# Softplus evictions gathered at the end of step 8, two products put later, one more tile on VectorE, and fewer rows of xh

## The reference, cut to what matters

```
xh, z = split(x @ W_in)                 # 512 channels each
xc = depthwise_conv_3x3(xh)             # 'SAME' padding
dt_r, Bp, Cp = split(xc @ W_xproj)      # 8, 16, 16
dt = softplus(dt_r @ W_dt + b_dt)       # 512 channels
dtN = dt @ W_dtN + b_dtN                # 16 states
for each pixel t, each channel, each of 16 states n:
    h[n] = exp(dt * A[n]) * h[n] + dtN[n] * Bp[n] * xc
    y    = sum over n of h[n] * Cp[n]  + Dskip * xc
y = layernorm(y) * silu(z) @ W_out + b_out
```

## Time and profile before

| what | value |
|---|---|
| time, median of 3 runs | 4421.09 us (4414.24 to 4431.68) |
| the profiled execution: its time, its span | 4415.12 us, 4413.4 us |
| VectorE busy | 4047.4 us, 92% of the span |
| GpSimd busy | 3843.1 us, 87% |
| TensorE busy | 3540.8 us, 80% |
| ScalarE busy | 3411.3 us, 77% |
| mean granted clock of TensorE | 0.922 |
| scan, L1041, 1536 of them | 2731.6 us |
| activation table loads, 385 of them | 1283 ns each |

### The profile page before, as it was taken

The page is one execution under the profiler, slowest core; times in us unless marked ns, Lnnn a source line. Parts: engine busy times, 40 slices in busy tenths (PEclk is TensorE's granted clock), DMA queues, the critical chain, the costliest instruction groups (busy, mean ns, idle before and its releaser), DMA issues.

```text
span 4413.4 us, 64194 instructions
## 1 busy us (share of the span) xinstructions
PE 3540.8 (80%) x20244; PEld 2225.9 (50%) x20244; DVE 4047.4 (92%) x4017; ACT 3411.3 (77%) x5782; POOL 3843.1 (87%) x2518
## 2 busy tenths in 40 slices
PE   6787888888887788877888778887887788878876
PEld 3454555555555555545554555454554555445544
DVE  3999999999999999999999999999999999999996
ACT  4778787777877787777787777887787777878774
POOL 4999999889998899888999889988899888998894
PEclk8899999998999999999899999999999899999987
DMA  5233223322233223322232223222232223222310
GB/s 132 65 97 100 65 69 100 91 87 62 85 92 92 79 61 103 91 79 75 83 102 73 79 72 101 86 75 76 89 105 65 75 82 105 83 61 80 100 54 22
DMA packets 189295, 363.22 MB, mean 82 GB/s; under 512 B 27416, under 2 KB 164120, under 8 KB 188960
## 3 DMA queue, kind: packets, MB, share of 16 engines
q1 hardware_dynamic: 188960, 359.12, 27.7%
HBM read 289.84 MB, written 69.21 MB: 81 GB/s over the span
## 4 chain that ended last, share of the span: by engine, by line
DVE 26%; ACT 23%; PE 20%; issue 18%; POOL 12%; DVEq 0%; DMA 0%; POOLq 0%; ACTq 0%; SPq 0%
DVE st L1041 18%; POOL st L599 10%; PE ht L1190 8%; ACT decay L727 6%; DVE y L1017 3%; ACT L918 3%; ACT weighed L756 3%; PE work L1227 2%; ACT dt L799 2%; ACT L799 2%; PE work L1262 2%; PE work L1232 1%; PE work L1163 1%; ACT xb L878 1%; PE work L1222 1%
## 5 line engine op out<-in xcount | busy, mean ns | idle before, releaser
L1041 DVE TENSOR_TENSOR_SCAN st<-decay,st 128x1024 f32<-128x1024 f32 (+1 forms) x1536 | 2731.6, 1778 | 138.6 <-ACT decay L727 101.0
L599 POOL TENSOR_TENSOR st<-xc,bbc 128x1536 f32<-128x1536 f32 x768 | 2652.0, 3453 | 56.1 <-DMA bbc<-brow 46.9
L727 ACT ACTIVATE decay<-dt,neg_a 128x1024 f32<-128x1024 f32 (+1 forms) x1536 | 1356.8, 900 | 413.4 <-DVE st L1041 410.7
L1190 PE MATMUL ht<-ident,st 128*128 128x128 f32 x9216 | 1348.5, 297 | 337.1 <-DVE st L1041 299.9
L1190 PEld LDWEIGHTS ht<-ident,st 128*128 128x128 f32 x9216 | 1134.6, 153 | 648.8 <-DVE st L1041 465.1
L1017 DVE SCALAR_TENSOR_TENSOR y<-ht,ct,y 128x512 f32<-128x512 f32 x1536 | 1119.9, 729 | 89.8 <-PE ht L1190 89.4
L632 POOL TENSOR_TENSOR y<-y,weighed 128x512 f32<-128x512 f32 x672 | 854.4, 1271 | 340.3 <-ACT weighed L756 336.1
L756 ACT ACTIVATE weighed<-ht,ct 128x512 f32<-128x512 f32 x672 | 459.4, 684 | 274.1 <-PE ht L1190 271.7
L1227 PE MATMUL work<-xn,win 128*128 128x384 f32 x768 | 344.6, 594 | 136.7 <-DVE volt L997 103.2
L1163 PE MATMUL work<-tri,conv_w 96*32 96x384 f32 x4608 | 415.6, 493 | 5.2 <-issue 2.0
L1222 PE MATMUL work<-xn,win 128*128 128x480 f32 x768 | 359.9, 593 | 4.6 <-ACT xn L850 3.2
(11 more groups left out here) (109 smaller groups left out, 3173.2 us busy)
## 6 DMA issues: line engine op xcount, KB each, us to landing
bbc<-brow SPq DMA_DIRECT2D x192, 768.0 KB, 6.1
tri<-rows_of_xh SPq DMA_DIRECT2D x576, 200.0 KB, 3.9
rows_of_xh<-xhp SPq DMA_DIRECT2D x192, 250.0 KB, 2.4
out_dram<-ot SPq DMA_DIRECT2D x43, 384.0 KB, 4.2
xin<-in_x_dram SPq DMA_DIRECT2D x42, 384.0 KB, 3.4
st<-in_x_dram SPq DMA_DIRECT2D x6, 384.0 KB, 5.5
out_dram<-y SPq DMA_DIRECT2D x4, 384.0 KB, 2.6
brow<-xp SPq DMA_DIRECT2D x48, 24.0 KB, 1.5
```

The lines of the kernel that those rows point to most:

```text
L599: u = g.tensor_tensor(slot, xc[:, kq % 2, :, :], bbc[:, piece_slot(kq, p), n % PIECE, :].unsqueeze(1).to_broadcast([P, DC, T]), ALU.mult)
L727: a.activation(flat(decay[:, :, :])[:, lo:hi], flat(dt[:, (k + ahead) % 2, :, :])[:, lo:hi], ACT.Exp, scale=neg_a[:, n:n + 1]).then_inc(s_ ...
L1041: v.tensor_tensor_scan(state[:, lo:hi], flat(decay[:, :, :])[:, lo:hi], state[:, lo:hi], 0.0 if h == 0 else state[:, lo - 1:lo], ALU.mult, ...
L1190: last = t.transpose(ht[:, m, c * P:(c + 1) * P], st[:, j, c, m * P:(m + 1) * P], ident[:, :])
```

## The change

- The four softplus evictions stand together at the end of step 8 with one pair of table loads. The products dt0 and dt1 stay at the end of step 7; dt2 and dt3 go to step 9, behind its transposes and ahead of l0 and l1.
- State 8 joins the table `OWN`: its tile 2 goes to VectorE.
- The first of the two membrane copies in step 9 stands ahead of `next_decay`.
- `TIN_STEPS` is (0, 6) in place of (6, 8).
- A chunk's xh is made only for the 8 rows that the chunk before did not have (384 columns), except for an image's first chunk, with 10. Rows in DRAM are kept for a whole image, and the normalised input xn loses a row that nothing reads.

```diff
-TIN_STEPS = (6, 8)
+TIN_STEPS = (0, 6)
...
-OWN = (10, 11,)
+OWN = (8, 10, 11,)
...
     7: ([(PRE, "ct")], [(PRE, "dt0"), (PRE, "dt1")], []),
-    8: ([], [(PRE, "dt2"), (PRE, "dt3")], []),
+    9: ([], [], [(PRE, "dt2"), (PRE, "dt3")]),
...
-                sp.dma_start(rows_v[c], xhp[:, c % 3, :, :].rearrange("p r w -> p (r w)")).then_inc(s_put[c], 16)
+                kq = (k + 1) % K
+                r0 = 0 if kq == 0 else TAPS - 1
+                sp.dma_start(rows_v[c][:, (kq * ROWS + r0) * WP:((kq + 1) * ROWS + 2) * WP],
+                             xhp[:, c % 3, r0:, :].rearrange("p r w -> p (r w)")).then_inc(s_put[c], 16)
...
-                    r0, r1 = (W if kx == 0 else 0), (HALO - W if kx == K - 1 else HALO)
+                    r0, r1 = W, (HALO - W if kx == K - 1 else HALO)
...
+                    taken = [(kc, h) for kc, a0_step in (L1_SLOTS.get(k, ()) if L1 in do else ())
+                             for h in range(CH) if s == l1_step(a0_step, h)]
+                    if s == BOTH_AT:
+                        for kc, h in taken[:1]:
+                            copy_membrane(kc, h)
                     next_decay(s)
...
+                    for kc, h in taken[1:] if s == BOTH_AT else taken:
+                        copy_membrane(kc, h)
                     for kind, name in late:
-                        if kind in do:
+                        if kind in do and name[:2] != "dt":
                             evacuate(name, kind)
-                    if s in (7, 8) and pre or s in (10, 11) and post:
+                    if s == 8 and pre:
+                        for c in range(DC):
+                            evacuate(f"dt{c}", PRE)
+                    if s == 8 and pre or s in (10, 11) and post:
                         a.preload_act_table_set(TABLES)
...
+                            lo = 0 if kc == K - 1 else (TAPS - 1) * W
                             for h in range(CH):
-                                last = t.matmul(work[:, i, 0:HALO], win[:, h, c * P:(c + 1) * P],
-                                                xn[:, (kc + 1) % 3, h, :], start=h == 0, stop=h == CH - 1)
+                                last = t.matmul(work[:, i, 0:HALO - lo], win[:, h, c * P:(c + 1) * P],
+                                                xn[:, (kc + 1) % 3, h, lo:], start=h == 0, stop=h == CH - 1)
```

More of the change, by code:

```diff
@@ L262, in vssm_lif_kernel @@
         brow = nc.dram_tensor("brow", [NS, T], F32).ap()
-        rows_v = nc.dram_tensor("rows_of_xh", [DC, P, (ROWS + 2) * WP], F32).ap()
+        rows_v = nc.dram_tensor("rows_of_xh", [DC, P, (H + 2) * WP], F32).ap()
         s_w = sem("weights_loaded")
@@ L455, in get_rows @@
                 hold("sp", sp, b)
+                top = (k + 1) % K * ROWS
                 for dy in range(TAPS):
                     sp.dma_start(tri[dy * Q:(dy + 1) * Q, c % 2, :, :, :].rearrange("i g r w -> i g (r w)"),
-                                 rows_v[c].rearrange("(g i) e -> i g e", i=Q)[:, :, dy * WP:(dy + ROWS) * WP]
+                                 rows_v[c].rearrange("(g i) e -> i g e", i=Q)[:, :, (top + dy) * WP:(top + dy + ROWS) * WP]
                                  ).then_inc(s_tri[c], 16)
@@ L780, in evacuate @@
                         i = await_filled(act, bc, kc, name)
-                        a.activation(xhp[:, c % 3, :, 1:1 + W],
-                                     work[:, i, 0:HALO].rearrange("p (r w) -> p r w", w=W),
+                        r0 = 0 if kc == K - 1 else TAPS - 1
+                        a.activation(xhp[:, c % 3, r0:, 1:1 + W],
+                                     work[:, i, 0:HALO - r0 * W].rearrange("p (r w) -> p r w", w=W),
                                      ACT.Copy).then_inc(emptied[i], 1)
```

## The result

The changed kernel takes 4441.02 us (median of 10 runs, 4433.88 to 4447.18). The kernel before took 4424.00 in the 10 runs beside it. The ratio is 1.0039, 95% interval 1.0029 to 1.0049: slower by 17 us, by less than the 0.5% bound, and 33 us above the predicted 4408. It lies in the range. The profiled execution has a span of 4438.8 us and a mean granted clock of 0.915.

The account below looks back on a forecast made before the run. It took VectorE, busy 92% of the span, as the bound, but ScalarE from scan 8 to 10 in chunk 0. Gain 43 less 30 for the clock is 13 us: 4408 us on the median's scale, range 4370 to 4452.

Parts of the forecast that it names:

- The chain in chunks 0, 4 and 5: Scan 8 to scan 10, serial from table load to decay: 11.6 us, 11.4 in chunk 5.
- State 8's tile: Third tile of state 8 on VectorE: 0.66 us, hidden in chunks 0, 4, 5, on the path in 1 to 3.
- The chain in chunks 1 to 3: Scan 8 to scan 10 with the spiking layer: l0 waits behind dt3, TensorE's chain sets the end, 14.4 us.
- The input transposes: Moved to step 0: no cost there beyond 1.01 us of bn_stats in step 1; higher clock worth 6 us.
- the sum: Whole change at full clock: 33 us from six images, 3.4 from image 0, 0.6 from image 7, 6 at step 0: 43.
- Eight rows of xh: A fifth fewer columns in products, evictions and writes: taken as nothing, between no effect and a few us.
- TensorE's clock: Scans 8 to 10: dt products and l0 partly at 1.2 GHz on the path, losing 30 us; the least known term.
- The price per chunk: At 1.2 GHz, scans 8 to 10: 1.37 us more for dt2 and dt3, 2.63 more with l0.
- the 91 us: Loss in scans 8 to 10 if all blocks run at 1.2 GHz: 26 x 1.37 + 21 x 2.63.
- The shares: Time at the lower level in scans 8 to 10: half in chunks 0, 4, 5, a fifth in 1 to 3.
- The net: Whole kernel: 43 us gained less 30 lost to the clock, so 13 us faster.
- The slower rival: Scans 8 to 10: two dt products and l0 on the path, all at 1.2 GHz; 4469 us, chance 0.20.

Follow-up runs that it names:

- the three kernels with fillers: The changed kernel with three, eight or fourteen unused products of 128 columns in step 8, behind its transposes: 4420.03, 4416.06 and 4402.85 us.
- the ungathered one: Kernel before with moved input transposes, eight-row xh and early membrane copy: 4364.92 us; with state 8's last four transposes made three times in chunks 1 to 3: 4343.46.

## Why the prediction was wrong, by its own steps

- **The chain in chunks 0, 4 and 5** was right: 11.55 and 11.43 at full clock for 11.6 and 11.4. Step 8 has 4.66 to 4.92 us in all chunks but one, and step 9 nearly all the waiting. State 8's tile is hidden there.
- **The chain in chunks 1 to 3** was right in its order and at full clock (14.38 to 14.43 in the eight chunks of the three kernels with fillers that show it), with l0 as what ends it.
- **The input transposes** were right: 513 us for scans 0 to 2, 512 predicted, with the clock up to 1.00 there. The fall of chunk 2's stretch from 17.44 to 14.4 that the sum gave to the whole change is brought by this part alone (14.30 in image 4). The sum put no price on each part: its 613 us for scans 8 to 10 at full clock are what the kernel without the gathered evictions and the tile takes, so even at full clock these two were worth nothing in sum.
- **Eight rows of xh**: nothing expected, 3 us measured, within the uncertainty.
- **TensorE's clock is the step that failed**, the sentence "with these shares 36 x 0.51 + 55 x 0.21 = 30 us go". The price per chunk was right: 12.92 less 11.55 is 1.37, and 17.03 less 14.40 is 2.63. The number of chunks was not. Scans 8 to 10 should have taken 613 us at full clock (671 - 37 - 21) and took 686: 73 of the 91 us went, not 30. Chunks 1 to 3 of images 1 to 7 have a mean of 16.74, so 21 x 2.34 = 49 of their 55 us, where the prediction took a fifth; the other 24 us are two thirds of the 36, where it took half. The shares came from the granted clock of the old stretches, which takes in idle time: of the 47 pairs dt2, dt3 in that trace only the one of the earlier trace rows was at 2.92. And in those stretches dt2, dt3 and, in chunks 2 to 4, six input transposes stood inside step 8. The change takes just that work away, so those rows told of a TensorE that would no longer be there. Most of the 3.81 us of idle time could have been foreseen: the transposes of a step wait for its scan, the prediction had step 8 at 4.7 us, and step 8 would have nothing else.
- **The net**: -13 predicted, +17 measured between the medians and +25 between the profiled executions. Of the 38 us between -13 and +25 the clock took 43 above its term, and scans 10 to 13 gave 9 back; the rest, with the 4 us of the later first scan, is 4. What makes up those 9 us was not separated; the kernel with the input transposes alone has 6 of them.

The slower rival named this mechanism. It put the point from which the kernel is slower by over 0.5% at 71% of the blocks; 34 of 47 pairs (72%), and 73 of the 91 us (80%), went, and the kernel came out 0.39% slower. It had 0.20; a count of what TensorE keeps in step 8 would have given it most. The rule of the Trainium skill ("TensorE: Matmul & The Clock Gate", section "HAM oscillation — how this bites in real kernels"), bursts parted by waits that start at the lower level again and again, would have taken all 91 us; the runs agree with it for 73.

Left open: whether adding work ahead of l0 in the gathered kernel would bring all its chunks 1 to 3 to 14.4. This was tried only in the ungathered one. Open too is what sets the level from chunk to chunk: l0 held it in four chunks with eight products, and in one with fourteen.

## What to carry to other kernels

A granted clock belongs to the work that stood in that stretch: when a change moves TensorE's work out of a step, list what is left there and how long TensorE then waits, and price everything behind it on the serial path at the lower level. Gathering saves the engine that issues the loads, but here a block of four evictions over two banks put a round trip to TensorE into the chain, so the wait that it removed came back longer. Run the parts of a compound change alone: here one line was worth 50 us, and another part cost more than that.

## What was not expected of the hardware

- The level can differ between two neighbouring groups of products: with 14 unused products in step 8 the dt pair took 1.55 us at a clock of 1.00, and l0 directly behind it ran in a stretch at 0.56; ahead of the pair TensorE had been idle for 1.02 us, with the clock at 1.00.
- Work that computes nothing can shorten a kernel: eight repeated transposes, 1.04 us of TensorE in a wait of over 2, took 21 us off (4364.92 to 4343.46).
